# Narrow layers of a four-layer cross-attention kernel: the output projection's quarter moves between two score tiles, one step later

## The reference

```
wide:    q = x @ Wq; k = ctx @ Wk; v = ctx @ Wv
         logits = q.k / 8 + column bias of two token pairs (masks A and B)
         x = x + softmax(logits) @ v @ Wo + bo
narrow:  xn = x * rsqrt(mean(x*x) + 1e-5) * norm_w
         q = xn @ wq; k = ctx @ wk; v = ctx @ wv      (each key head serves 4 heads)
         x = x + softmax(q.k / sqrt(32)) @ v @ wo
```

## Time and profile before

| | us |
|---|---|
| median of three timed runs | 2085.48 (2083.67 to 2086.32) |
| the profiled execution's own time | 2084.65 |
| its span, first to last instruction | 2082.9 |
| PE busy in the span | 2041.1 (98%) |
| DVE, ACT, POOL busy | 1390.1, 965.1, 644.0 |
| mean granted TensorE clock | 0.998 of 2.4 GHz |

### The profile page before, as it was taken

How to read it: one execution, slowest core, us unless ns; L and a number is a source line. 1 busy time by engine, 2 the same in 40 slices (tenths; PEclk the granted TensorE clock), 3 DMA queues, 4 the chain that set the end, 5 groups by cost and what they waited for, 6 DMA issues and landing times.

```text
span 2082.9 us, 31293 instructions
## 1 busy us (share of the span) xinstructions
PE 2041.1 (98%) x11546; PEld 1763.6 (85%) x11546; DVE 1390.1 (67%) x2408; ACT 965.1 (46%) x1814; POOL 644.0 (31%) x519
## 2 busy tenths in 40 slices
PE   8999999999999998999999999999999989999998
PEld 8999988888888887788888888888888867888886
DVE  5332365775568556788888676557755675888885
ACT  3222353553445344565554554335534553555552
POOL 1000042321232255454443341223222543444441
PEclk9999999999999999999999999999999999999999
DMA  7999842222122223343333332212221222333322
GB/s 192 187 173 197 190 96 63 72 64 75 51 71 73 66 65 87 84 108 95 92 89 92 104 97 65 77 52 72 65 75 51 81 79 66 82 91 89 81 71 83
DMA packets 262393, 191.02 MB, mean 92 GB/s; under 512 B 197506, under 2 KB 199970, under 8 KB 259682
## 3 DMA queue, kind: packets, MB, share of 16 engines
q1 hardware_dynamic: 262242, 189.03, 36.0%
HBM read 132.66 MB, written 56.26 MB: 91 GB/s over the span
## 4 chain that ended last, share of the span: by engine, by line
PE 89%; DVE 6%; DMA 1%; ACT 1%; issue 1%; SPq 1%; POOL 0%; DVEq 0%; ACTq 0%
PE acc_bank L865 11%; PE acc_bank L255 8%; PE acc_bank L257 8%; PE acc_bank L256 8%; PE q_bank L823 8%; PE q_bank L825 8%; PE q_bank L827 8%; PE t_bank L845 7%; PE ctx_bank L255 3%; PE ctx_bank L256 3%; PE ctx_bank L257 3%; PE s_bank L786 2%; PE s_bank L255 2%; PE s_bank L783 2%; PE s_bank L789 2%; PE s_bank L257 2%
## 5 line engine op out<-in xcount | busy, mean ns | idle before, releaser
L1299 POOL TENSOR_TENSOR prob<-prob,rinv 128x1232 f32<-128x1232 f32 x128 | 288.3, 2252 | 1023.4 <-DVE rinv L1183 1023.4
L1043 ACT ACTIVATE q_s<-q_bank 128x512 fp32r<-128x512 f32 x192 | 114.8, 598 | 520.5 <-PE q_bank L827 516.3
L865 PE MATMUL acc_bank<-pT_s,vals_s 128*128 128x512 f32 x1024 | 338.1, 416 | 0.0
L1141 DVE TENSOR_REDUCE mx<-s_bank 128x4 f32<-128x308 f32 x512 | 240.5, 470 | 123.8 <-PE s_bank L257 63.9
L823 PE MATMUL q_bank<-x_s,w_s 128*128 128x512 f32 x768 | 318.7, 415 | 4.0 <-POOL w_s L1292 4.0
L827 PE MATMUL q_bank<-x_s,w_s 128*128 128x512 f32 x768 | 313.0, 408 | 0.0
L825 PE MATMUL q_bank<-x_s,w_s 128*128 128x512 f32 x768 | 312.6, 407 | 0.0
L255 PE MATMUL acc_bank<-o_s,w_s 128*128 128x512 f32 x752 | 303.6, 404 | 2.5 <-DVE o_s L1174 2.5
L257 PE MATMUL acc_bank<-o_s,w_s 128*128 128x512 f32 x752 | 296.8, 395 | 0.0
L256 PE MATMUL acc_bank<-o_s,w_s 128*128 128x512 f32 x752 | 296.7, 395 | 0.0
L1145 DVE TENSOR_TENSOR prob<-s_bank,mx 128x308 f32<-128x308 f32 x512 | 245.1, 479 | 27.4 <-DVE mx L1141 1.4
(11 more groups left out here) (107 smaller groups left out, 4091.3 us busy)
## 6 DMA issues: line engine op xcount, KB each, us to landing
stream<-x_back SPq DMA_DIRECT2D x128, 256.0 KB, 2.6
x_front<-stream SPq DMA_DIRECT2D x96, 256.0 KB, 3.4
x_back<-stream SPq DMA_DIRECT2D x96, 256.0 KB, 3.9
kvw_raw<-kvw SPq DMA_DIRECT2D x17, 1024.0 KB, 8.4
k_scr<-k_out SPq DMA_DIRECT2D x36, 308.0 KB, 10.6
keys_s<-k_scr SPq DMA_DIRECT2D x128, 77.0 KB, 2.5
v_scr<-v_out SPq DMA_DIRECT2D x8, 1024.0 KB
vals_s<-v_scr SPq DMA_DIRECT2D x512, 6.5 KB
```

The lines of the kernel that those rows point to most:

```text
L865: mm = pe.matmul(out, w, pT_s[:, part], start=i == mine[0] and part == 2 * n and w is v[0], stop=i == mine[-1] and w is terms[-1][0] and p ...
L1141: dve.tensor_reduce(top, scored, AX_X, ALU.max).then_inc(s_max, 1)
L1299: pool.tensor_tensor(view, view, rinv[:, slot].unsqueeze(2).broadcast_to([P, TILES * GH, CTX]), ALU.mult).then_inc(p_norm, 1)
```

## The change

1. `Plan.projections`: in the narrow layers (all batches but the layer's last, and but batch 30) a quarter comes one step later: batch `gb`'s first in step `4 gb + 6`.
2. `Plan.ahead` is now true in every narrow step whose quarters belong to a batch that had its last values two steps ago. That makes it true in steps 38 to 63, 102 to 124, 126 and 127, besides 34 and 98.
3. In such a step with one quarter, PE computes it between the second and the third score tile, where half of the queries stood; all 12 query matmuls (24 in step 63) come behind the first transposes.
4. DVE's `add_result` for that quarter stands at the same place of the order as before, behind the four score tiles, but is now that of the same step; `acc_bank` entries swap order (quarter, then values). SP stores it at the end of the step instead of behind the next step's keys.

At the edges: steps 37 and 101 lose their quarter. Step 64 has one as before, step 65 three instead of two, step 125 two instead of one, of which batch 30's first is still put off by `late`.

```
     def ahead(self, s):
-        return 2 * GROUPS <= s < NU and s % (2 * UNITS) == UNITS + 2
+        found = self.projections(s) if s < NU and kind(s).name == "B" else []
+        return bool(found) and GROUPS * found[-1][0] + GROUPS - 1 < s - 2
...
                 if layer % 2 and b < B - 1:
-                    at += m
+                    at += m + (gb < BATCHES - 2)
...                                                       (PE, narrow step)
                     run(scores(s, 1), 1)
-                    run(q, half)
+                    between = plan.ahead(s) and len(plan.projections(s)) == 1
+                    if between:
+                        for gb, m in plan.projections(s):
+                            project(gb, m)
+                    else:
+                        run(q, half)
                     run(scores(s, 2), 1)
                     run(scores(s, 3), 1)
-                    if plan.ahead(s):
+                    if plan.ahead(s) and not between:
                         for gb, m in plan.projections(s):
                             project(gb, m)
                     run(v, 3)
                     turned(0)
-                    run(q, half)
+                    run(q, 2 * half if between else half)
                     run(v, 9)
...                                                       (DVE, narrow step)
                     if plan.ahead(s):
-                        denominators(s)
+                        if len(plan.projections(s)) == 2:
+                            denominators(s)
                         for gb, m in plan.projections(s):
                             add_result(gb, m)
                     turned(0)
-                    if s < NU and not plan.ahead(s):
+                    if s < NU and not (plan.ahead(s) and len(plan.projections(s)) == 2):
                         denominators(s)
```

## The result

| | us |
|---|---|
| after, median of 13 runs | 2089.73 (2088.62 to 2091.24) |
| before, median of 13 runs on the same chips | 2085.44 (2083.67 to 2087.14) |
| ratio after to before | 1.0024, 95% interval 1.0016 to 1.0031 |
| after, the profiled execution | 2090.99, span 2089.2, mean granted clock 0.996 |

The change made the kernel slower by 4.3 us in the medians and by 5.0 us by the ratio, whose interval gives 3.3 to 6.5 us. The time lies inside the predicted range, 2.7 us above the predicted 2087.0. It also lies 0.03 us above the 2089.7 from which the prediction would have called the kernel slower, and just outside the 2084 to 2089.6 that it held most likely.

The account below looks back on a forecast made before the run. PE's own queue was taken to set the time (busy 98%). Terms -4.4 + 1.6 + 1.3 + 2.3 + 0.7 = +1.5 us on the median 2085.48 gave 2087.0; range 2081.5 to 2092.5, most likely 2084 to 2089.6 (0.67).

Parts of the forecast that it names:

- ordinary step: Full narrow steps 38 to 62 and 102 to 124: 0.14 us gained less 0.05 mean wait, 48 times, -4.4 us.
- steps 37 and 101: Into steps 38 and 102: first scores wait 0.8 us for DVE's query part, twice, +1.6 us.
- step 125: Old order meets a later DVE: third and fourth tile wait 1.45 us instead of 0.10, +1.3 us.
- step 126, the wait: Values wait 2.4 us for the put-off `add_result` of batch 30's first quarter, less 0.1 before: +2.3 us.
- step 126, the clock: Clock falling to half after the new 2.4 us wait: one chance in four, +1.7 us, not in the sum.
- step 127: Values behind the step lose the quarter as cover and wait for the last transposes' part: +0.7 us.
- the step without a wait: Ordinary step if DVE keeps up: 10.38 us against 10.52, taken from step 63's 10.29 plus 0.09.
- the +3.2 us: The sum by the Trainium skill's rule that long enough idle gaps halve PE's clock, instead of +1.5.
- Rival 1: Ordinary step's fourth tile: DVE 0.2 us later, mean wait 0.22, +9.7 us, 2095; chance 0.20 in full form.
- Rival 2: Waits of steps 125 and 126 hidden, ordinary step keeps all 0.14: -4.4 us, 2081.1; chance 0.08.
- Rival 3: SP's queue becomes the bound, steps stay at 10.52 and the edges remain: +5.9 us, 2091.4; chance 0.05.
- Rival 4: Third tile may never have waited for DVE; only the fourth tile's 0.10 us counts, already in the sum; no chance given.

Follow-up runs that it names:

- e5: Changed kernel, but step 125 has its older quarter between second and third score tile, the younger at its end, each added in its place: 2084.99 us, ratio 0.9997.
- e1: Changed kernel, but DVE adds step 125's second quarter (batch 30's first) at the end of step 125, not in step 126: 2086.35 us, ratio 1.0005.
- e8: Changed kernel with six query matmuls kept beside the quarter, so 18 matmuls between second and third score tile: 2139.1 us, ratio 1.0262.
- e6: Kernel before, no quarter moved, seven instead of six query matmuls between second and third score tile: 2079.67 us, ratio 0.9975.
- e3: Changed kernel with the new order in layer 1 only, layer 3 as before: 2084.09 us, ratio 0.9996.

## Why the prediction was right, and by how much it was off

The forecast (no change, 2087.0 us) had the mechanism and the sign of each term, and its range held. The size of the whole was missed: +1.5 us forecast, +4.3 measured in the medians, at the very edge of what the prediction would still call no change. Step by step:

| term of the sum | predicted | in the traces |
|---|---|---|
| ordinary step, 48 times | -0.09 each, -4.4 | -0.067 each, -3.2 |
| steps 37 and 101 | +1.6 | +1.4 (0.72 and 0.70) |
| step 125 | +1.3 | +1.5 (e5: 1.4) |
| step 126, the wait | +2.3 | +2.2 (2.38, less 0.17 that e1's step is shorter than before's) |
| step 126, the clock | 1 in 4, left out | +1.65 (e1) |
| step 127 | +0.7 | +0.8 |
| sum | +1.5 | +4.4 |
| medians; ratio | | +4.3; +5.0 (3.3 to 6.5) |

**The ordinary step** was mis-sized. The wait came out as worked: in a step that follows one with `stats` it is gone, in the others the fourth tile's first two matmuls start 0.17 to 0.19 apart (1005.26, 1005.45 in the timeline of PE), where the undisturbed distance is 0.14 (1004.85, 1004.98), so 0.03 to 0.05 is left, less than the 0.07 of the prediction. What was wrong is the step without a wait, 10.38. I took it from step 63, which has queries in both places. In step 50 the twelve matmuls of the quarter take 1002.05 to 1004.85 = 2.80, 0.233 each, and the steps that follow one with `stats`, which have no wait left, last 10.43: 0.05 more than I took from step 63. A stand-in of the same count but of another kind of matmul was good to 0.05 us, and that times 48 is 2.4 us, over half of the gain I claimed. Only half of it shows in the sum (1.2 us), since the smaller wait that was left made up for the rest: that is luck.

**The edges** were right within 0.2 us each. The four numbers for step 126 stand in the trace nearly as worked out: third tile taken by DVE at 4.29 in the step (4.21), `add_result` ended at 6.78 (6.70), PE released at 6.88 (6.85), wait 2.38 (2.4).

**The clock** is the term I left out. I gave its fall one chance in four, since no row showed what a wait of 2.4 us does. It fell, for the same 3.4 us at 0.50 as in the earlier trace rows, and cost 14.39 - 10.36 - 2.38 = 1.65 us. With the ordinary step's 1.2 this is the whole distance between the two sums. The prediction also called the known gap one of 2.7 us; in the trace it is one idle stretch of 2.51 and one of 0.20, so the new one (2.21 us idle) was nearer to it than it seemed, and I should have given the fall more than a quarter.
The rule of the Trainium skill weighed there (TensorE: Matmul & The Clock Gate, "HAM oscillation — how this bites in real kernels") says that idle gaps put PE back to half its clock if they are long enough. Taken at its word it spoke against a fall here and not for it, as the gaps that the Trainium skill warns of there are longer than either of these; the +3.2 us that the prediction drew from the rule read it too freely. The measurement decides: in after PE was busy for 0.59 of 2.80 us, and then the clock stood at 0.50.

**The rivals.** Rival 1 (DVE comes back later than added up) fell: it wanted a mean wait over 0.10, and DVE came at 2.07 instead of 2.05. Its mechanism is real, as e8 shows, 1.4 us further on. Rival 2 (the edges cost little) fell with e1 and e5, which find 2.4 and 1.4 us in the two edges it wanted hidden. Rival 3 (SP falls behind) fell: steps got shorter while its stores moved, and no wait on a DMA stands in PE's list. Rival 4 (the third tile never waited for DVE) was right and already in the sum; that the fourth tile did wait is shown by e6, where one matmul of cover took 0.10 us out of the step.

What is left open: in how many runs of after the clock falls in step 126. The medians, ratios and mean clocks of e1 and after suggest most, and e8 shows that it needn't. Step 127's edge was read from the trace alone; no run takes it away.

## What to carry to other kernels

A wait of 0.1 us that a matmul has inside its own record appears in no list of waits and is worth 5 us when it comes 48 times; find it by the distance of starts, and cover it with just as much work as it is long (here one matmul), since work taken from another place uncovers what it hid there. Moving a whole block to a later step pays at each end of the software pipeline: before the change, list for the first and last steps who frees the bank that the next entry takes, above all where an operation is put off by a step. Many small waits gathered into one long one are not the same sum, because the long one can take the clock with it.

## What the runs showed of the hardware

The clock's falls at the entries into the narrow layers aren't a property of the code alone. Before has them at 794.4 and 1698.9, after at 779.4, 806.7, 1683.9 and 1701.0, each 3.41 us long at 0.50. At about 1681.5 PE waits 1.98 us for POOL's `w_s`, in both traces at the same time to 0.01 us and with the same instructions. Windows of after there:

```profile
1680.00:1683.90 3.90, 1.92 (x14) 1.61 (x14) 3.20 (x6) 3.89 (x9) 3.08 (x3) 1.00 0.09 13
1683.90:1687.30 3.40, 3.40 (x13) 2.92 (x12) 1.55 (x4) 0.69 (x2) 2.22 (x1) 0.51 0.59 177
```

and of before in the same times:

```profile
1680.00:1683.90 3.90, 1.92 (x14) 1.61 (x14) 3.21 (x6) 3.89 (x9) 3.08 (x3) 1.00 0.09 12
1683.90:1687.30 3.40, 3.40 (x22) 2.95 (x20) 2.70 (x6) 1.11 (x3) 2.23 (x1) 1.00 0.58 162
```

PE is busy for 1.92 us in both, and the clock falls in one and stays in the other. The ten traces hold 20 such waits for `w_s`, each of 1.97 to 1.99 us idle, and seven were followed by a fall within 2 us; of the 22 idle stretches of 2.04 to 2.71 us, 20 were, and one of the two that weren't is e8's step 126. This is where the profiled execution of after has its 1.09 us in steps 63 to 95 (1140.33 to 1694.54 = 554.21, where e3, with the same instructions there, has 1139.30 to 1692.38 = 553.08 and no fall, and e1, with a fall at 1683.0, has 554.29). Such a fall shifts a single execution by about 1 us, a quarter of what was to be measured here: a pair of profiles can't be compared by their spans, only step by step.
